# Adjacency product with layer norm on one core: sixteen chunks of 512 nodes through two 64 KB pieces, TensorE's program inside a loop of two turns

## The reference

```
keep = (u >= 0.1)
x_drop = x * keep / (1 - 0.1)
y = x + adj @ x_drop                      # adj is 8192 x 8192, x is 8192 x 64, all fp32
out = (y - mean(y)) / sqrt(var(y) + 1e-5) # mean and variance over the 64 columns of a row
```

## Time and profile before

| | value |
|---|---|
| median of 3 runs | 641.97 us (641.90 to 642.12) |
| the profiled execution's own time | 641.88 us |
| its span, first to last instruction | 640.1 us |
| mean granted TensorE clock | 0.922 |
| TensorE matmuls busy | 502.8 us, 79% |
| VectorE busy | 53.7 us, 8% |
| ScalarE busy | 17.7 us, 3% |
| DMA | 274.84 MB, mean 429 GB/s |

### The profile page before, as it was taken

The page is one execution under the profiler, slowest core; times in us unless marked ns, Lnnn a source line. Parts: engine busy times, 40 slices in busy tenths (PEclk is TensorE's granted clock), DMA queues, the critical chain, the costliest instruction groups (busy, mean ns, idle before and its releaser), DMA issues.

```text
span 640.1 us, 5097 instructions
## 1 busy us (share of the span) xinstructions
PE 502.8 (79%) x2312; PEld 179.7 (28%) x2312; DVE 53.7 (8%) x102; ACT 17.7 (3%) x41; POOL 1.6 (0%) x14
## 2 busy tenths in 40 slices
PE   0097969688799578879878689867869868689997
PEld 0062213232233222223222223222323223133344
DVE  1930001010010100101000010100101001010101
ACT  0001000000000000000000000000000000000000
POOL 1000000000000000000000000000000000000000
PEclk9997979988799978889979899978999969799999
DMA  9999999999999999999999999999999999999998
GB/s 393 459 394 455 431 420 454 405 446 439 422 421 436 435 451 422 438 408 444 459 418 434 442 412 455 420 434 446 426 418 426 446 451 422 438 405 438 425 425 364
DMA packets 7207, 274.84 MB, mean 429 GB/s; under 512 B 800, under 2 KB 928, under 8 KB 1312
## 3 DMA queue, kind: packets, MB, share of 16 engines
q1 hardware_dynamic: 7056, 272.63, 98.8%
q10 hardware_dynamic: 144, 2.10, 0.8%
HBM read 272.63 MB, written 2.10 MB: 429 GB/s over the span
## 4 chain that ended last, share of the span: by engine, by line
DMA 62%; PE 33%; DVE 3%; another core or an unknown queue 1%; issue 0%; ACT 0%; SPq 0%; DVEq 0%; ACTq 0%
DMA ring<-adj 56%; PE acc L202 33%; DMA ring<-adj_last 5%; DMA xdrop<-u 2%; DVE node_sum L317 1%; DVE xdrop L321 1%; DVE xdrop L329 1%; PE folded L210 0%; DVE x_sb L321 0%; PE lifted L237 0%; SPq L126 0%; ACT squares L303 0%; PE lifted L263 0%; ACT std L308 0%
## 5 line engine op out<-in xcount | busy, mean ns | idle before, releaser
L202 PE MATMUL acc<-ring,xdrop 128*64 128x512 f32 (+1 forms) x2176 | 485.6, 606 | 103.1 <-DMA ring<-adj 101.7
L202 PEld LDWEIGHTS acc<-ring,xdrop 128*64 128x64 f32 x2176 | 162.8, 146 | 413.0 <-issue 280.2
L344 DVE SCALAR_TENSOR_TENSOR y<-folded,x_sb 128x256 f32<-128x256 f32 (+1 forms) x16 | 6.7, 416 | 552.3 <-PE folded L210 552.3
L237 PE MATMUL lifted<-x_sb,lift 128*128 128x64 f32 x4 | 1.1, 428 | 30.6 <-DVE x_sb L321 30.6
L210 PEld LDWEIGHTS folded<-fold,sums_T 128*128 128x128 f32 x128 | 15.5, 191 | 12.6 <-issue 12.6
L284 ACT COPY sums_T<-acc 128x512 f32<-128x512 f32 x15 | 8.8, 585 | 335.0 <-PE acc L202 335.0
L210 PE MATMUL folded<-fold,sums_T 128*128 128x64 f32 x128 | 17.7, 281 | 0.0
L277 ACT ACTIVATE std<-square_sum,eps 128x4 f32<-128x4 f32 (+1 forms) x16 | 4.8, 297 | 225.2 <-DVE square_sum L351 225.2
L237 PEld LDWEIGHTS lifted<-x_sb,lift 128*128 128x128 f32 x4 | 0.9, 322 | 30.5 <-issue 30.5
L348 DVE TENSOR_TENSOR squares<-y 128x256 f32<-128x256 f32 (+1 forms) x16 | 6.7, 417 | 0.5
L355 DVE TENSOR_TENSOR x_sb<-y,rstd 128x256 f32 (+1 forms) x16 | 6.7, 416 | 0.6
(11 more groups left out here) (23 smaller groups left out, 5.5 us busy)
## 6 DMA issues: line engine op xcount, KB each, us to landing
ring<-adj SPq DMA_DIRECT2D x13, 4096.0 KB, 31.3
ring<-adj SPq DMA_DIRECT2D x2, 2048.0 KB, 28.7
xdrop<-u ACTq DMA_DIRECT2D x1, 2048.0 KB, 12.5
x_sb<-x SPq DMA_DIRECT2D x1, 2048.0 KB, 12.3
out<-x_sb SPq DMA_DIRECT2D x1, 1984.0 KB, 12.7
ring<-adj_last SPq DMA_DIRECT2D x1, 1920.0 KB, 29.5
ring<-adj_last SPq DMA_DIRECT2D x1, 1792.0 KB, 33.4
ring<-adj_last SPq DMA_DIRECT2D x1, 1536.0 KB, 30.6
```

The source lines that it names most:

```text
L202: last = nc.tensor.matmul(acc[i][D * h:D * h + D, 0:cols], xdrop[:, k, :], piece[:, b, :], start=(k < 2), stop=(k >= NB - 2))
L344: nc.vector.scalar_tensor_tensor(out=y[:, 0:nj, :], in0=folded[:, 0:nj, :], scalar=1.0 / KEEP, in1=x_sb[:, bass.ds(block0, nj), :], op0=AL ...
```

## The change

All 16 chunks are 512 wide now and are computed in order. There is no ring: two buffers (`pieces`) of 32 blocks, 64 KB per partition each, 128 KB together. Chunk c is piece 0 (blocks 0 to 31) and piece 1 (blocks 32 to 63). The load of a piece waits until TensorE has used the same buffer's last piece entirely. Only the last chunk's pieces are loaded in parts: two for the first (19 and 13 blocks), seven for the second (9, 7, 6, 4, 3, 2, 1). TensorE waits for these parts' semaphores in every turn; GpSimd raises them in advance for the turns in which nothing is loaded in parts.

There is one accumulator. TensorE waits at the start of each chunk until ScalarE has copied the sums of the one before, and folds them between piece 0 and piece 1. ScalarE's and VectorE's loops take one chunk a turn, fifteen turns, and nothing comes ahead of them. The last chunk, four groups of 128 nodes instead of two, goes through the `lifted` path.

TensorE's program stands in an `If(turn > 0)` inside a `Fori(0, 2)`: in the first turn it is jumped over.

```diff
-NARROW = 2
+NARROW = 1
...
-RING = 5
...
-ACC_OF = (0, 1, 0, 1, 2)
...
-PARTS = (15, 14, 12, 9, 6, 5, 3)
+PARTS = ((19, 13), (9, 7, 6, 4, 3, 2, 1))
...
-        ring = sb("ring", [P, RING * HALF, COLS])
+        pieces = [sb(f"piece{s}", [P, PB, COLS]) for s in range(SLOTS)]
...
-        acc = [pb(f"acc{i}", [P, COLS]) for i in range(3)]
+        acc = pb("acc", [P, COLS])
...
+            for s in range(SLOTS):
+                load(0, s)
+            with sp.Fori(1, CHUNKS - 1) as c:
+                for s in range(SLOTS):
+
+                    sp.wait_ge(piece_used, c * SLOTS + (s + 1 - SLOTS))
+                    load(c, s)
+            for s in range(SLOTS):
+                sp.wait_ge(piece_used, FINAL * SLOTS + s + 1 - SLOTS)
+                for n, (k, size) in enumerate(parts[s]):
+                    arrived = part_in[s][n - 1] if n else piece_in[s]
+                    sp.dma_start(pieces[s][:, k:k + size, :], adj_last[s, :, k:k + size, :]).then_inc(arrived, 16)
...
+            def multiply(c, s):
+
+                for n, (k0, size) in enumerate(parts[s]):
+                    if n:
+                        pe.wait_ge(part_in[s][n - 1], c * 16 + 16)
+                    else:
+                        pe.wait_ge(piece_in[s], c * 16 + 16)
+                    for b in range(k0, k0 + size):
+                        k = s * PB + b
+                        h = k % 2
+                        last = nc.tensor.matmul(acc[D * h:D * h + D, :], xdrop[:, k, :], pieces[s][:, b, :],
+                                                start=(k < 2), stop=(k >= NB - 2))
+                last.then_inc(piece_used, 1)
+
+            def program():
...
+                with pe.Fori(0, CHUNKS) as c:
+
+
+                    pe.wait_ge(sums_copied, c + 1)
+                    multiply(c, 0)
+                    for j in range(J):
+                        last = nc.tensor.matmul(folded[:, j, :], sums_T[:, j * P:j * P + P], fold[:, :],
+                                                start=True, stop=True)
+                    last.then_inc(folded_ready, 1)
+                    multiply(c, 1)
+                for j in range(LAST_J):
+                    pe.wait_ge(last_copied, j + 1)
+                    nc.tensor.matmul(lifted[:, j, 0:D], sums_T[:, j * P:j * P + P], fold[:, :],
+                                     start=False, stop=True).then_inc(last_folded, 1)
+
+
+            with pe.Fori(0, 2) as turn:
+                with pe.If(turn > 0):
+                    program()
...
+            with act.Fori(0, FINAL) as c:
+                act.wait_ge(piece_used, c * SLOTS + SLOTS)
+
+                act.wait_ge(folded_ready, c + 1)
+                nc.scalar.copy(sums_T[:, :], acc[:, :]).then_inc(sums_copied, 1)
                 spread(c)
...
+            act.wait_ge(piece_used, CHUNKS * SLOTS)
+            act.wait_ge(folded_ready, CHUNKS)
             for j in range(LAST_J):
-                act.wait_ge(folded_ready, FINAL + 1 + j)
+                nc.scalar.copy(sums_T[:, j * P:j * P + P], acc[:, j * P:j * P + P]).then_inc(last_copied, 1)
```

More of the change, by code:

```diff
@@ L19 @@
 LAST_SLOTS = NB // LAST_PB
[L20 to L31 removed]
+FINAL = CHUNKS - 1
+QUARTERS = 4
+QB = NB // QUARTERS
+BANK = 512
 P_DROP = 0.1
@@ L34 @@
 EPS = 1e-5
-PARTS = (15, 14, 12, 9, 6, 5, 3)
+PARTS = ((19, 13), (9, 7, 6, 4, 3, 2, 1))
+LATE = sum(len(sizes) - 1 for sizes in PARTS)
 def graph_layernorm(nc, x, adj, adj_last, u, out):
@@ L71, in graph_layernorm @@
         rstd = sb("rstd", [P, J])
-        acc = [pb(f"acc{i}", [P, COLS]) for i in range(3)]
+        acc = pb("acc", [P, COLS])
         folded = pb("folded", [P, J, D])
[L75 to L89, removed]
+        lifted = pb("lifted", [P, LAST_J, BANK])
+        parts = [[(sum(sizes[:n]), size) for n, size in enumerate(sizes)] for sizes in PARTS]
+        piece_in = [sem(f"piece_in{s}") for s in range(SLOTS)]
+        part_in = [[sem(f"part_in{s}_{n}") for n in range(1, len(parts[s]))] for s in range(SLOTS)]
         x_in = sem("x_in")
         u_in = sem("u_in")
-        half_used = sem("half_used")
-        last_done = sem("last_done")
+        piece_used = sem("piece_used")
         sums_copied = sem("sums_copied")
-        half_copied = sem("half_copied")
+        last_copied = sem("last_copied")
+        last_folded = sem("last_folded")
         folded_ready = sem("folded_ready")
@@ L121, in _ @@
             sp.dma_start(x_sb[:, :, :], x[:, :, :]).then_inc(x_in, 16)
[L123 to L167, removed]
+            def load(c, s):
+                sp.dma_start(pieces[s][:, :, :], adj[c * SLOTS + s, :, :, :]).then_inc(piece_in[s], 16)
@@ L176, in _ @@
         def _(pool):
-            for n in range(2):
-                nc.gpsimd.memset(late_free[:, n:n + 1], 0.0).then_inc(late_in[n], (ROWS // (2 * RING) - 1) * 16)
+            for n, arrived in enumerate(part_in[0] + part_in[1]):
+                nc.gpsimd.memset(late_free[:, n:n + 1], 0.0).then_inc(arrived, FINAL * 16)
+            nc.gpsimd.memset(sums_T[:, :], 0.0).then_inc(sums_copied, 1)
             nc.gpsimd.memset(eps[:, :], EPS).then_inc(eps_ready, 1)
@@ L196, in _ @@
         def _(pe):
[L197 to L231, removed]
@@ L234, in _ @@
[L234 to L260, removed]
@@ new lines, in program @@
+            def program():
+                pe.wait_ge(lift_ready, 1)
+                pe.wait_ge(x_centred, 1)
+                for j in range(LAST_J):
+                    nc.tensor.matmul(lifted[:, j, 0:D], lift[:, :], x_sb[:, NB - LAST_J + j, :],
+                                     start=True, stop=False)
+                pe.wait_ge(fold_ready, 1)
+                pe.wait_ge(dropped, QUARTERS)
+                with pe.Fori(0, CHUNKS) as c:
[6 more added lines that the diff above has]
+                    multiply(c, 1)
+                for j in range(LAST_J):
+                    pe.wait_ge(last_copied, j + 1)
+                    nc.tensor.matmul(lifted[:, j, 0:D], sums_T[:, j * P:j * P + P], fold[:, :],
+                                     start=False, stop=True).then_inc(last_folded, 1)
@@ L319, in centre @@
                 dve.wait_ge(node_sum_ready, n)
-                sums = node_sum[:, which, quarter(q)].unsqueeze(2).to_broadcast([P, HALF, D])
+                sums = node_sum[:, which, quarter(q)].unsqueeze(2).to_broadcast([P, QB, D])
                 nc.vector.scalar_tensor_tensor(out=out[:, quarter(q), :], in0=sums, scalar=-1.0 / D,
@@ L327, in _ @@
             dve.wait_ge(u_in, 16)
-            for q in range(HALVES):
+            for q in range(QUARTERS):
                 nc.vector.scalar_tensor_tensor(out=xdrop[:, quarter(q), :], in0=xdrop[:, quarter(q), :], scalar=P_DROP,
@@ L333, in _ @@
                 centre(xdrop, xdrop, q, q + 1, 0, dropped)
[L335 to L345 removed]
+            for n, q in enumerate((QUARTERS - 1, *range(QUARTERS - 1))):
+                centre(x_sb, x_sb, q, QUARTERS + n + 1, 1, x_centred)
@@ L346, in normalise, with per_row @@
+            dve.wait_ge(x_centred, QUARTERS)
+            def per_row(v):
+                return v[:, :].unsqueeze(2).to_broadcast([P, J, D])
+            def normalise(c, block0):
+                dve.wait_ge(folded_ready, c + 2)
+                nc.vector.scalar_tensor_tensor(out=y[:, 0:J, :], in0=folded[:, 0:J, :],
+                                               scalar=1.0 / KEEP, in1=x_sb[:, bass.ds(block0, J), :],
                                                op0=ALU.mult, op1=ALU.add).then_inc(y_ready, 1)
@@ L358, in normalise @@
                 dve.wait_ge(rows_ready, c + 1)
-            normalise(0, NB - J, nj=LAST_J)
-            with dve.Fori(1, CHUNKS) as c:
-                normalise(c, (c - 1) * J)
+            with dve.Fori(0, FINAL) as c:
+                normalise(c, c * J)
             dve.wait_ge(std_ready, FINAL + 1)
```

46 lines of the change are left out of this document (11 added, 35 removed).

## The result

The changed kernel takes 663.9 us (median of 6 runs, 657.1 to 671.2), against 641.8 for the kernel before (6 runs, 641.7 to 642.1). The ratio is 1.032, with an interval of 1.028 to 1.037. It is slower, as forecast, but by 22 us instead of 5.5, and outside the range (644.4 to 651.0). One of its six runs, the one at 671.2, is a slow one; the other five lie between 657.1 and 665.1, still 8 us apart, where those of before lie within 0.4.

A forecast was written before the change was run, and what follows sets the result against it. Bound by the DMA stream of 32 rows, 19.36 us apart: piece 29 landed at 593.9, TensorE ended at 640.4, span 645.5, plus 1.8 outside the trace, 647.3 us. Own range 644.6 to 650.5; 8 in 10, 644.4 to 651.0.

The forecast's parts named there:

- The reload: Two-buffer loads: starting one costs 1.6 us, the longest piece leaves 2.4 us, so the stream is not broken.
- The starved stream: Rival, DMA queue: late loads taking 3 us to start delay a third of 30 pieces, +5, 652; chance 0.12.
- The piece's length: TensorE's work on one piece: 13.95 us plus 0 to 3.0 for lost clock, 1.6 taken, longest 17.0.
- The pass over the program: TensorE's jumped-over first turn: takes an instruction packet out of the stream; if not, 1.0 us more.
- The copy and its table load: ScalarE's work between chunks: 2.0 us together, hidden in the middle, on the path only behind piece 29.
- A fetch at the loop's back edge: Rival, TensorE's loop in 16 turns: at most 1.6 us left at the last chunk's head, 648.9; chance 0.05.
- The end: Last chunk: TensorE starts piece 29 at 593.9, ends at 640.4, some 7 us behind the last byte; span 645.5.
- Keeping step: Rival, last chunk: the parts reach TensorE in time, span 639.3, 641.1 in all, 0.9 under before; chance 0.06.
- The forecast's own range: Whole time, from clock loss, the held-up engine and the table load, none tied: 644.6 to 650.5.

The follow-up runs named there:

- e5: Changed kernel, each piece loaded as 4 blocks, issued when the old first 4 are used, and 28 blocks issued as late as before: 654.4 us.
- e8: Changed kernel, each piece loaded as 2 blocks, issued when the old first 2 are used, and 30 blocks issued as late as before: 657.9 us.
- e3_before_late: Kernel before, with each row loaded half a row later, when TensorE has used up the whole row before last: 657.1 us.
- e4: Changed kernel with one extra square root on ScalarE ahead of its loop, so that no table load stands inside the loop: 662.8 us.
- e7: e6 with TensorE's program written once, without the loop of two turns: 645.5 us.
- e6: Changed kernel, pieces loaded as two halves, each reloaded as it comes free, TensorE starting on each half as it lands: 645.5 us.
- e9: e6 with the second half of piece 30 in the last chunk loaded in parts of 7, 5, 3 and 1 blocks: 644.8 us.

## Why the prediction was wrong

**The step that failed is "The reload".** It took what it costs to start a load from two rows of a queue that was empty or alone (1.6 us for the last store, 2.6 for x), set it against the least time left (2.4 us), and concluded that the stream is not broken: a delay of 0 in the sum. The trace shows 12 us in its place. In a stream that keeps all engines busy that price is too low. In the changed kernel's trace I set each of the 28 reloads of whole pieces that follow the first two against the time from its issue to the last landing of the piece before:

| time left, us | reloads | mean delay, us | largest |
|---|---|---|---|
| under 2.5 | 2 | 1.3 | 1.9 |
| 2.5 to 3.5 | 6 | 0.6 | 1.8 |
| 3.5 to 4.5 | 10 | 0.35 | 1.1 |
| 4.5 to 5.5 | 8 | 0.3 | 1.2 |
| over 5.5 | 2 | 0.0 | 0.1 |

So the bound is not 1.6 or 2.6. In this trace it lies near 5.5, with only two reloads above; in e5 and e8 no late load lost over 0.1 us from 4.8 on. The last landing is not the best point to count from, for the engines finish a piece 1.1 to 3.0 us apart. Counted from issue to the first landing of the piece before, the 16 reloads with 2.5 us or less hold 10.3 of the 12 us, and none of the 12 with more came over 0.4 late; in e5 the least is 2.8. The first landing itself comes late as x had suggested: with 0.1 to 1.7 us left to it, it is 0.7 to 1.9 us late. What the prediction had no term for is that other engines come later still. The packets show two parts of it: DMA engines idle between two pieces (at 405 to 407 us only 12 to 15 packets are under way instead of 16), and 64 KB packets that take up to 4.19 us where the median is 2.42. What the 64 KB packets took above their median adds up to 9.1 us per engine in the changed kernel, 7.4 in e3_before_late, 0.5 in the kernel before.

**The starved stream** was among the rivals, at 12%, with a price of 5 us. It names the right wait, a load that starts late, but not its size nor where it strikes: I counted a third of the pieces at 0.5 us, some 5 in all, and only pieces of over 16.4 us. It was 13 of 28 with over 0.35 us, five of them over 1, 12 in all; the three reloads behind pieces of over 16.4 us hold 3.7 of it, the others fell on ordinary pieces. What should have warned me was in the prediction itself: "no load before was ever issued so late". The 14.5 us that I read off one load is not the least of the kernel before: there the least is 9.3 us (issued at 62.9, the row ahead lands at 72.2). But it held no row for a load with 2 to 7 us left, and I used the nearest row as if it were a bound.

**The piece's length** was right: 13.95 to 16.93 us. It matters through the reload now. Where the clock fell, the piece was used up late, the reload came late, TensorE waited longer. That the runs lie 8 us apart fits with this, if the clock falls at other places in each; it isn't shown, for the runs without a profile do not say where. The trace of e4, whose loads wait as in the changed kernel, has other lengths and another take-up of piece 29 (610.87).

**The pass over the program** did not do what I took it for. Six of the seven instruction packets are gone, but e7, without the pass, has only one as well: they went with the program's new form. The pass moved the one that is left, to 4.45 us, into the load of x, and the first piece came at 33.66 instead of 32.50. I had taken the packet to be fetched before the first transfer. e7 shows that the net is zero.

**The copy and its table load**: 2.12 measured, 2.0 predicted, once on the path. There is no drain behind the load: 623.00 plus 1.28 is 624.28, and the copy starts at 624.30. The measurement decides against the 1.4 us that the Trainium skill (ScalarE: Activation LUTs, What ACT_TABLE_LOAD costs) would have added. A fetch at the loop's back edge was not seen either: the trace has no instruction packet of 16 KB but the one at 4.45 us, and the pause of the last chunk is all ScalarE's.

**The end** was right in mechanism and nearly in size: 51.6 predicted from piece 29's take-up to the span's end, 53.5 measured. Of the 1.9 us, 1.7 are piece 30's own loss of clock (15.65 instead of 13.95), which I had put into the range and not into the sum. The backlog was 8.2 us behind the last landing (647.4) instead of 7. The tail behind the last product was 2.9 to the store's issue, as predicted.

**Keeping step** (the rival on the other side) is what e6 and e9 build, with the last product 2.3 and 1.3 us behind the last landing, and it needed a change of the waits in all chunks.

**The forecast's own range**, 644.6 to 650.5, does not follow from the terms given for it: added up they make 644.4 to 651.5. The result lies outside either way, because the reload had no term in it.

## What to carry to other kernels

Count for each transfer how much issued work lies in the queue when it is issued, and compare the least of these, not their mean, with what the loaded queue needs. Here it was 5 to 6 us to the last landing, or some 3 to the first, and cutting off a small first part of the next load (4 of 32 blocks) bought it all, without more memory. A price taken from an idle queue is not a bound for a full one. At the end of a stream ask from which wait on the consumer was last free to start: parts of the last load help only a consumer that is not a whole piece behind.

## What the runs showed of the hardware

- With 16 DMA engines at 64 KB packets, a load issued 3.5 us before the last engine is dry can land 1.8 us late. The Trainium skill (DMA: Bandwidth & Descriptors, Latency and other measured facts) gives 0.6 us to the first byte for transfers issued by SyncE, and 2 us for memory access at high load; the first would have allowed this reload. Both together, 2.6, are near what the first landings show: eight reloads that came 0.7 to 1.9 us late there moved 1.7 to 2.8 us behind their issue, an estimate from the landings less the 19.36 of a piece; the last landings want more. Why one engine starts so much later than the others stays open: no run took the descriptor's way apart from the data's.
- An engine that is ahead of the last loses only its lead, as I assumed: with only 3.0 us left the reload landing at 171.48 was not delayed on the last engine, while the first engine came 1.9 late.
- Splitting a transfer of 64 KB per partition costs 0.07 us per piece in a queue that is full, and an instruction packet of 16 KB holds one engine up by 1.0, early or late.
